# Depthwise first taps on ScalarE, a two-tensor mask for the k mean, loads in two groups, new orders and PSUM slots

## The reference

```python
# layer 0: attention in windows of 8x8 pixels, 4 heads, then a gated 3x3 convolution
scores = einsum('bhnd,bhmd->bhnm', q, k) / sqrt(d)
attn = softmax(scores + bias)                       # bias by relative position
x = x + windows_back((attn @ v) @ proj_w.T + proj_b)
a, b = split(w1 x + w1_b)
g = a * sigmoid(b)                                  # border repeated
y = leaky_relu(conv3x3(g, w2_w) + w2_b, 0.2)
x = x + y
# layer 1: linear attention with depthwise convolutions (6 heads)
x = x + dwconv(x, cpe1_w, cpe1_b)
y = ln2d(x)
act_res = silu(conv1x1(y, act_proj_w, act_proj_b))
y = conv1x1(y, in_proj_w, in_proj_b)
t = silu(dwconv(y, dwc_w, dwc_b))                   # "dwc"
q, k = elu(t @ qk_w.T + qk_b) + 1;  v = t
z = 1 / (q . mean(k) + 1e-6)                        # the k mean
kv = rope(k).T @ v / n
attn = (rope(q) @ kv) * z + dwconv(v, lepe_w, lepe_b)   # "lepe"
x = x + conv1x1(attn * act_res, out_proj_w, out_proj_b)
x = x + dwconv(x, cpe2_w, cpe2_b)
x = x + fc2(gelu(fc1(ln2d(x))))
```

## Times and profile before

| | |
|---|---|
| median of 3 runs | 798.58 us (796.69 to 803.7) |
| the profiled execution | 797.02 us, of it the span 795.0 us |
| mean granted PE clock in it | 0.959 of full speed |
| PE busy | 92% of the span |
| DVE busy | 67% |
| ACT busy | 57% |
| POOL busy | 39% |
| chain that ended last | PE 58%, DVE 22%, issue 6%, POOL 5%, ACT 4%, SPq 4%, DMA 1% |

### The profile page before, as it was taken

One profiled execution on the slowest core, in us unless ns is written; L12 is line 12 of the kernel. 1 busy time (PEld: TensorE's weight loads), 2 busy tenths in 40 slices (PEclk: granted clock), 3 DMA queues, 4 the chain that ended last, 5 costly groups with the idle time before them and its releaser, 6 DMA issues.

```text
span 795.0 us, 19684 instructions
## 1 busy us (share of the span) xinstructions
PE 732.6 (92%) x8424; PEld 463.3 (58%) x8424; DVE 533.7 (67%) x677; ACT 450.0 (57%) x638; POOL 309.4 (39%) x230
## 2 busy tenths in 40 slices
...
GB/s 60 33 68 16 2 31 2 2 2 15 1 16 17 32 31 31 16 32 1 31 31 46 21 27 2 2 2 31 32 16 1 27 22 16 1 31 1 43 5 45
...
## 3 DMA queue, kind: packets, MB, share of 16 engines
...
q10 hardware_dynamic: 512, 0.04, 0.1%
...
## 4 chain that ended last, share of the span: by engine, by line
PE 58%; DVE 22%; issue 6%; POOL 5%; ACT 4%; SPq 4%; DMA 1%; ACTq 0%; DVEq 0%; POOLq 0%
PE ps L590 21%; DVE QS L1178 9%; PE ps L580 7%; PE ps L681 5%; PE ps L837 4%; DVE CT L1192 3%; PE ps L656 3%; PE ps L667 3%; PE ps L765 2%; SPq L468 2%; PE ps L810 2%; PE ps L827 2%; DVE SC L1122 1%; PE ps L635 1%; PE ps L644 1%
## 5 line engine op out<-in xcount | busy, mean ns | idle before, releaser
L1331 POOL TENSOR_TENSOR SC<-SC,mx 128x768 f32<-128x768 f32 x48 | 77.2, 1609 | 172.5 <-DVE mx L1126 172.5
L590 PE MATMUL ps<-XP,wdw 48*64 48x384 f32 x1728 | 144.0, 483 | 0.0
L1192 DVE SCALAR_TENSOR_TENSOR CT<-TP,vec_sb,CT 112x768 f32<-112x768 f32 x96 | 123.6, 1304 | 1.3
L590 PEld LDWEIGHTS ps<-XP,wdw 48*64 48x64 f32 x1728 | 68.1, 132 | 69.4 <-issue 56.6
L1178 DVE SCALAR_TENSOR_TENSOR QS<-XP,vec_sb,QS 112x768 f32<-112x768 f32 x96 | 104.8, 1133 | 0.5
L1122 DVE TENSOR_TENSOR SC<-ps,bias_sb 128x768 f32<-128x768 f32 x48 | 45.7, 953 | 54.6 <-PE ps L656 54.1
L590 PE MATMUL ps<-G,w_sb 48*64 48x384 f32 x864 | 73.8, 493 | 1.3 <-ACT QH L1018 1.3
L681 PEld LDWEIGHTS ps<-vx,PT 128*128 128x128 f32 x576 | 66.6, 192 | 9.0 <-issue 5.5
L681 PE MATMUL ps<-vx,PT 128*128 128x52 f32 x576 | 68.8, 275 | 0.8 <-DVE XP L1152 0.4
L1023 ACT ACT_TABLE_LOAD x53 | 68.0, 1283 | 0.9
L1336 POOL TENSOR_TENSOR XP<-XP,YB 112x768 f32<-112x768 f32 x12 | 22.4, 1870 | 110.2 <-DMA YB<-YF 110.2
...
## 6 DMA issues: line engine op xcount, KB each, us to landing
...
wln_sb<-in_const_dram SPq DMA_DIRECT2D x6, 9.0 KB
```

Of the source, the lines that this page charges most:

```text
L590: mm = pe.matmul(slot(job)[half(c, HALF), r * BANK:r * BANK + SPX], w[half(r), tap * HALF:(tap + 1) * HALF], shifted(t, d * CROWS + c * WI ...
L1192: dve.scalar_tensor_tensor(out=ct, in0=win, scalar=wt, in1=ct, op0=ALU.mult, op1=ALU.add).then_inc(lepe_step, 1)
L1331: pool.tensor_tensor(sc, sc, bc_last(mx[:, (u % NSC) * 12:(u % NSC) * 12 + 12], TOK), ALU.subtract).then_inc(sub_ready, 1)
```

## The change

1. The first tap of each of the 24 depthwise convolutions (12 dwc, c10; 12 lepe, c20) is an activation Identity with scale and bias on ACT. Two semaphores, dwc_begun and lepe_begun, tell DVE's tap 1 that it is there. The jobs c10 and c20 stand in ACT_ORDER and are gone from DVE_ORDER.
2. km_sb is a SCALAR_TENSOR_TENSOR: head blocks x PSUM column x head blocks. The factor 1/PX is folded into a column of eye2_sb once, in DVE's s2.
3. The 37 loads become 24 on loaded_b and 13 on a new loaded_c (wout, swap, wfc2, rope_y, rope_x, twice each, masks, rope_th, rope_tw). Only DVE's z0 waits for loaded_c. The x strips 3, 4 and 5 of pair 0 are issued between and behind the loads of loaded_b.
4. All five orders, the PSUM slots and the places of the keep-busy matmuls are other ones. The calls of L837 are 242 instead of 222; 87 instead of 67 of them stand ahead of q.3.0, and 155 behind it in both. The table loads that the planner places are 48 instead of 53.

```diff
-        N_V, N_QK, N_A, N_W, N_B = 2, 8, 6, 8, 37
+        N_V, N_QK, N_A, N_W, N_B, N_C = 2, 8, 6, 8, 24, 13
...
-            for t in range(3, STRIPS):
-                load(0, t)
...
+                load(0, 3 + b)
...
+            load(0, STRIPS - 1)
...
+                elif name == "c10":
+                    wait_read(act, ("ip", i, halo_last(n)))
+                    if i:
+                        wait_filled(act, ("at", i - 1, n))
+                    act.activation(rows16(T0[n]), shifted(XP[i % 2], n * CROWS, CROWS, TAPS[0])[0:RG], ACT.Identity,
+                                   scale=v(f"dwc_{TAPS[0]}"), bias=v("dwc_b")).then_inc(dwc_begun, 1)
+                elif name == "c20":
+                    act.wait_ge(t_ready, i * CH + halo_last(n) + 1)
+                    if kc >= 2:
+                        wait_filled(act, ("op", (kc - 2) // CH, (kc - 2) % CH))
+                    act.activation(rows16(CT[kc % 2]), shifted(TP, n * CROWS, CROWS, TAPS[0])[0:RG], ACT.Identity,
+                                   scale=v(f"lepe_{TAPS[0]}"), bias=v("lepe_b")).then_inc(lepe_begun, 1)
...
-                    dve.wait_ge(loaded_b, N_B * 16)
+                    dve.wait_ge(loaded_c, N_C * 16)
...
+                    dve.wait_ge(setup_pool, N_POOL)
+                    dve.tensor_scalar(eye2_sb[:, C:C + 1], eye2_sb[:, C:C + 1], 1.0 / PX, None, ALU.mult)
...
-                        dve.tensor_scalar(km_sb[:, to], head_blocks[:, 0:C], slot(job)[0:RG, at:at + 1],
-                                          1.0 / PX, ALU.mult, ALU.mult)
+                        dve.scalar_tensor_tensor(out=km_sb[:, to], in0=head_blocks[:, 0:C],
+                                                 scalar=slot(job)[0:RG, at:at + 1], in1=head_blocks[:, 0:C],
+                                                 op0=ALU.mult, op1=ALU.mult)
```

More of the change, by code:

```diff
@@ new lines @@
+    ar.0.1 ar.0.2 rs.1.0 x3.1.1 ie.1.0 x3.1.2 z.0.0 z.0.1 sq.1.1 z.0.2 rs.1.1 sq.1.2 c20.0.2 ar.1.0 ie.1.1
+    rs.1.2 ar.1.1 c10.1.0 ie.1.2 c10.1.1 c10.1.2 x4.0.0 sq2.0.0 ar.1.2 rs2.0.0 ge2.0.0 ge0.0.0 ge1.0.0 ts.1.0
+    x4.0.1 ts.1.1 c20.1.0 sq2.0.1 xw.2.0 xw.2.1 ts.1.2 c20.1.1 x4.0.2 ve.1.0 ve.1.1 sq2.0.2 rs2.0.1 rs2.0.2
+    ke.1.0 ke.1.1 kx.2.0 ge1.0.1 ge0.0.1 ge2.0.1 vx.2.0 kx.2.1 xw.2.2 ge2.0.2 ge1.0.2 ve.1.2 ge0.0.2 ex0.2.0
+    vx.2.1 xw.2.3 ex1.2.0 ex0.2.1 pt0.2.0 pt1.2.0 qe.1.0 qe.1.1 ex1.2.1 kx.2.2 ke.1.2 qe.1.2 pt1.2.1 oe.2.0
@@ new lines @@
+    ex0.3.1 kx.3.2 ex1.3.1 yf.2.1 sg.2.5 pt1.3.0 ed.2.5 vx.3.0 xw.3.2 ex0.3.2 yf.2.2 x3.2.0 oe.3.0 pt1.3.1
+    pt0.3.1 sq.2.0 kx.3.3 ex1.3.2 x3.2.1 rs.2.0 ex0.3.3 x3.2.2 ie.2.0 sq.2.1 sq.2.2 vx.3.1 rs.2.1 rs.2.2 xw.3.3
+    ie.2.1 pt0.3.2 c10.2.0 oe.3.1 pt1.3.2 ie.2.2 c10.2.1 sg.3.0 vx.3.2 ed.3.0 sg.3.1 c10.2.2 vx.3.3 ed.3.1
+    kx.3.4 xw.3.4 pt0.3.3 ar.2.0 xw.3.5 ex1.3.3 oe.3.2 kx.3.5 vx.3.4 pt1.3.3 ex0.3.4 ex1.3.4 sg.3.2 ed.3.2
+    ex0.3.5 pt0.3.4 pt1.3.4 vx.3.5 oe.3.3 ex1.3.5 pt0.3.5 pt1.3.5 ts.2.0 yf.3.0 oe.3.4 ts.2.1 ke.2.0 c20.2.0
@@ new lines @@
+    ve.2.0 ke.2.1 sg.3.3 oe.3.5 ts.2.2 ed.3.3 ve.2.1 c20.2.1 sg.3.4 qe.2.0 ed.3.4 ke.2.2 sg.3.5 qe.2.1 ed.3.5
+    ve.2.2 qe.2.2 yf.3.1 yf.3.2 ar.2.1 ar.2.2 x3.3.0 z.2.0 z.2.1 sq.3.0 z.2.2 x3.3.1 sq.3.1 rs.3.0 rs.3.1
+    c20.2.2 x3.3.2 ie.3.0 ie.3.1 sq.3.2 c10.3.0 x4.2.0 rs.3.2 ar.3.0 ar.3.1 sq2.2.0 ie.3.2 ar.3.2 rs2.2.0
+    c10.3.1 c10.3.2 ts.3.0 x4.2.1 ge1.2.0 ve.3.0 sq2.2.1 ge0.2.0 ge2.2.0 ke.3.0 rs2.2.1 ts.3.1 ts.3.2 x4.2.2
+    c20.3.0 c20.3.1 ge2.2.1 ge0.2.1 sq2.2.2 ve.3.1 ge1.2.1 ke.3.1 rs2.2.2 ve.3.2 ke.3.2 ge2.2.2 ge1.2.2 ge0.2.2
@@ L227, in spare, with begun @@
     return found
+def begun(text, prefix):
+    found = [(i, n) for name, i, n in jobs(text) if name == prefix]
+    return {t: j + 1 for j, t in enumerate(found)}
 def steps(text, prefix):
```

281 lines of the change are left out of this document (133 added, 148 removed).

## The result

The changed kernel takes 763.4 us (median of 4 runs, 762.0 to 765.4), the kernel before 801.1 (4 runs, 796.7 to 807.5): a ratio of 0.953, 95% interval 0.945 to 0.960. That is 37.7 us faster.

What follows compares the result with a forecast made beforehand. It took PE, busy 732.6 of 795.0 us, as the bound on average. From 797.0, terms -6.0, -5.0, -9.0, -4.0, 0, +5.2 and +1.0 gave 779.2; 1.6 up to the runs' median made 780.8 us, range 770 to 799.

Steps and rivals of the forecast that it cites:

- The first taps: 24 depthwise first taps, 21.2 us, leave DVE for ACT; said to count only where DVE makes PE wait.
- 200 to 207 us, -5.0: PE's 5.71 us wait for DVE's gate G and the slow convolution behind it: two thirds of 7.5 us gained.
- Pair 2, -9.0: 590 to 622 us: convolutions fill PE's waits before kv.2.2 and kk.2.0, removing waits and low clock, 9.0 us gained.
- The rest, -4.0: Waits at the k-v product and mask matmul elsewhere, 11.8 us: fillers gain a third, 4.0 us.
- Loads, -6.0: Setup: PE's 3.93 us wait for the rope table and 2.1 us of low clock behind it go.
- Mask, 0: The k mean's new mask form on DVE should wait for POOL as before: 0, bounds 0 and -8 us.
- rival B: Fillers cover nearly all waits, 771.3 us; second support: mask free, up to 8 us more, 772.8 us; chance 0.16.
- Keep-busy, +5.2: 20 more keep-busy matmul calls on PE at 0.26 us each cost 5.2 us if none replaces a wait.
- ACT, +1.0: First taps wait in ACT's list ahead of the next pair's LN work; one 0.90 us tap on the path, +1.0 us.
- The signs I had named: Checks: no rope-table wait, full clock after 40 us, taps 0.85 to 1.0 us; wrong if PE waits over 3 us for ACT.
- Rival D: ACT becomes the late engine through the added taps and the fillers bring nothing: slower, 807.9 us; chance 0.12.
- C: POOL bounds pair 2, so fillers only move the wait to the at jobs: 791.8 us; chance 0.24.

Runs made afterwards that it cites:

- e2: The changed kernel with only the 24 first taps back on DVE, directly ahead of the second taps: 787.7 us, ratio 0.981 to the kernel before.
- e14: The kernel before with 24 extra unused DVE maxima (17.4 us) ahead of the first taps: 821.9 us, ratio 1.029 to the kernel before.
- e5: The kernel before, own orders, with taps, loads and mask edits, two of the 24 taps moved up in ACT's list: 793.2 us, ratio 0.989.
- e4: The kernel before, own orders, with taps, loads and mask edits, taps on ACT as soon as their inputs are there: 818.1 us, ratio 1.018.
- e1: The changed kernel's orders, PSUM slots and keep-busy matmuls with the code edits for taps, loads and mask undone: 789.8 us, ratio 0.982 to before.
- e3: The changed kernel with one group of 37 loads behind the x strips, as before; z0 keeps its later place: 764.2 us.
- e16: The kernel before with only the loads split in two groups and z0 behind qb.0.4: 803.8 us against 800.6, ratio 1.003.
- e9: The changed kernel with the k mean's mask in its old form: 762.0 us.
- e8: The changed kernel without 62 keep-busy calls (ahead of ip.1.2, xc2.0.0, f12.0.0, d3.2.1): 767.7 us, ratio 0.955 to the kernel before.
- e12: The changed kernel with 1.4 us moved from DVE's setup block s2 into z0 and 8 more keep-busy calls ahead of sc0.0.4: 764.9 us.

## Why the prediction was wrong, step by step

**The first taps: the term that failed.** I counted 21.2 us that leave DVE and then gave them 3.7 us, inside the -5.0 of 200 to 207 us, on the argument that DVE counts only where PE waits for it by name. e2 shows 24 in the new orders, some 5 of it perhaps clock. A sign of it stood in the rows of before: DVE was busy for 19.96 of 20 us in a stretch in which PE had 15.49, and e14 shows that DVE's time was dear there. An engine that is full for a stage can set the stage's length also where PE's single waits are short and named after others. But no row of before gave the 24: in the old orders the same relief was worth 9 to 12 us with the best placing tried (e5) and less than nothing with the first (e4). That orders and taps bring more together than one by one has no term in my sum at all.

**200 to 207 us, -5.0.** The stage from d0.0.0 to kp.0.0 gained 14.0 us: 9.2 by the orders alone (15.4 lost in before, 6.2 in e1), the rest by the taps. The wait of 5.71 us for `G` is gone: no wait for `G` is among PE's waits in the changed kernel.

**Pair 2, -9.0.** From kt.2.0 to d3.2.0 before lost 19.6 us, e1 11.2 and the changed kernel 8.6: 8.4 by the orders, 11.0 with all. This term held. The mechanism was half right: with the convolution between them kv.2.2 waits no more, but POOL's list has changed too (pair 2's k ropes stand ahead of q ropes now), and how much each did was not separated.

**The rest, -4.0.** Pair 1 and the tail gained 13 us (from kp.0.0 to kt.2.0 18.4 to 9.1; behind d3.2.0 7.7 to 4.5). Nearly all of pair 1 came by the taps: e1 has 18.7 there and e2 16.9.

**Loads, -6.0.** The local reading was right, and the end did not move (e3, e16). Two steps failed. I priced the wait of 3.93 us as if PE's new order left it as it was, and with that order it is 0.68 us without the split (e3). And in the old orders the 5.7 us gained did not last: in the one trace of e16 a stretch at low clock behind 157 us took most of it. What makes such a stretch come is open.

**Mask, 0.** Held. In all kernels it takes 1.31 to 1.46 us on average in either form, and e9 ends where the changed kernel does. The rule of the Trainium skill, "SBUF — State Buffer", "Who interferes with whom", by which an instruction of VectorE with two SBUF inputs contends with a GpSimd instruction that reads SBUF, agrees with the 1.33 us of the new form; the 8 us of rival B's second leg were not there.

**Keep-busy, +5.2.** Priced at full length, where most stood in waits: e8 says 0 or less. **ACT, +1.0.** A tap takes 1.02 us, not 0.90; the estimate of 1.01 from the Trainium skill, "ScalarE: Activation LUTs", "What ACT_TABLE_LOAD costs", was the better one. The difference of 2.9 us on ACT moved nothing that the runs show.

**The signs I had named.** Held: no wait for the rope table, none over 2 us for `G`, kv.2.2 at 2.18 us, a clock of 0.92 in pair 2, the mask's length. Not held: the clock is at 0.91 in 40 to 60 us, and a tap takes 1.02 us. A wait of PE for ACT of more than 3 us, which was to be a sign of being wrong, is there too, 3.9 us for `kx`. It stands at 13 us, ahead of the first product of scores and of every tap, so it tells nothing of them.

So the sum came to -17.8 where -37.7 was measured. Without the terms for the loads and for ACT it has -12.8, near the 13 to 14 of the orders alone (e1): what I had summed was in the main the orders. By stages this is in part luck, for 200 to 207 us was set too low, e1 lost 4.4 us at the start, and pair 1 gained nothing by the orders. The range ended at 770 since rival B's best case had nothing of its own for the taps either. Rival D, slower by ACT's head of line, was real in e4 and depends on two tokens; C, POOL as the bound, did not come.

## To carry over

Find the engine that is full in a stage before pricing what leaves it: work taken off it can be worth its full time there, though PE never waits for it by name. How much of it arrives depends on the orders: the same taps were worth some 24 us in the new ones and 9 to 12 at best in the old ones, so a part should be priced in the kernel that it will stand in. An extra instruction put on an engine shows whether its time is dear; it measures what adding costs (21 us for 17.4 here), not what taking away gives. Follow a local gain to the end before counting it. Where two engines share an in-order chain, place the handed-over instruction ahead of anything that waits for a third; two tokens cost 23 to 25 us here.

## What the runs showed of the chip

- After the same wait of 2.39 us at 52 us the clock in 60 to 80 us was 0.75 in one kernel (e2) and 1.00 in another (the changed one), with nothing different ahead of it on PE; e12, whose wait there is 0.84 us, has 0.83, and e3, with waits of 0.68 and 1.46 us, has 1.00 from 40 to 80 us. So what a short wait costs varies by some 5 us from one traced execution to the next, more than several of the effects looked for here. What decides it is open.
- An activation from SBUF with scale and bias pointers over 112x768 takes 1.012 to 1.042 us in the changed kernel, within 3% wherever it stands; in the seven that ran beside a POOL instruction for 0.8 us or more it took 1.016 to 1.031. The same tap on VectorE took 0.67 to 1.84 in the kernel before.
- A scalar_tensor_tensor on one column of 32 rows took 1.46 us where it began 0.03 us behind a POOL instruction of 1.47 us, in the setup of the changed kernel. In the kernel before it began 0.05 us ahead of the same POOL instruction and took 0.15 us. The rows of the changed kernel, then of before:

```profile
43.35 1.47 POOL L1353 TENSOR_TENSOR SC<-SC,mx 128x768 f32<-128x768 f32 x1 [4.28 <-DVE mx L1156]
43.38 1.46 DVE L1113 SCALAR_TENSOR_TENSOR vec_sb<-last,vec_sb 32x1 f32<-32x1 f32 x1
...
45.84 0.15 DVE L1083 SCALAR_TENSOR_TENSOR vec_sb<-last,vec_sb 32x1 f32<-32x1 f32 x1
45.89 1.47 POOL L1331 TENSOR_TENSOR SC<-SC,mx 128x768 f32<-128x768 f32 x1 [9.12 <-DVE mx L1126]
```
